# A Winograd filter's leftover channels: copied from the transformed tile into four 32-row tiles, instead of from the raw tile into two 64-row tiles

## Time and profile before

| | |
|---|---|
| median of 3 runs | 13046.61 us (13036.51 to 13055.05) |
| the profiled execution's own time | 13046.61 us |
| its span in the profile | 13044.8 us |
| mean granted TensorE clock | 0.982 |
| busy share of the span: PE, DVE, ACT, POOL | 95%, 64%, 42%, 36% |
| the third layer's filters, first to last | 5219.3 to 9748.2 us of the span |
| DMA engines over the third layer, mean share | 61% |

### The profile page before, as it was taken

How to read it: one execution, slowest core, us unless ns; L and a number is a source line. 1 busy time by engine, 2 the same in 40 slices (tenths; PEclk the granted TensorE clock), 3 DMA queues, 4 the chain that set the end, 5 groups by cost and what they waited for, 6 DMA issues and landing times. The chain is left out here.

```text
span 13044.8 us, 315786 instructions
## 1 busy us (share of the span) xinstructions
PE 12434.4 (95%) x126170; PEld 8455.1 (65%) x126170; DVE 8394.4 (64%) x17482; ACT 5423.2 (42%) x11157; POOL 4731.3 (36%) x3557
## 2 busy tenths in 40 slices
PE   7999899899989998999999999999998999999998
PEld 6877433577767776555555555555547777787777
DVE  0000677433335544888888888888887777777777
ACT  0000111211223333444444444444446666666666
POOL 0000222000000154666666666666653343333343
PEclk9999999999999999999999999999999999999999
DMA  4333556883754597666666666666642222222222
GB/s 128 133 133 130 135 153 160 160 154 70 153 126 151 155 228 184 83 85 86 84 85 85 85 86 84 85 85 85 86 75 63 52 51 52 52 52 52 53 51 49
DMA packets 2310007, 1323.92 MB, mean 101 GB/s; under 512 B 1872228, under 2 KB 2219867, under 8 KB 2222959
## 3 DMA queue, kind: packets, MB, share of 16 engines
q1 hardware_dynamic: 2041484, 1201.47, 46.4%
q10 hardware_dynamic: 267232, 104.65, 3.4%
HBM read 648.72 MB, written 450.74 MB: 84 GB/s over the span
## 5 line engine op out<-in xcount | busy, mean ns | idle before, releaser
L1581 PE MATMUL l_m<-l_wa,l_pix 128*128 128x288 f32 x8192 | 2263.6, 416 | 39.8 <-DVE l_qkv L1770 22.0
L1439 POOL TENSOR_TENSOR l_qkv<-l_qkv,l_copies 128x576 f32<-128x576 f32 x1024 | 1437.4, 1404 | 1727.5 <-DVE l_qkv L1773 1366.1
L1581 PEld LDWEIGHTS l_m<-l_wa,l_pix 128*128 128x128 f32 x8192 | 1454.3, 190 | 799.0 <-issue 370.9
L1285 PE MATMUL l1h_ps<-l1h_ring,l1h_w 96*96 96x256 f32 x6120 | 1327.4, 379 | 50.1 <-ACT l1h_ring L1233 47.0
L1056 PE MATMUL l1v_ps<-l1v_rows,l1v_w 96*96 96x256 f32 x6120 | 1325.3, 378 | 33.5 <-ACT l1v_rows L1029 33.5
L1429 POOL TENSOR_TENSOR l_pix<-l_raw 128x516 f32<-128x516 f32 x1024 | 1299.2, 1269 | 24.7 <-DMA l_raw<-l_raw 24.7
L2091 PEld LDWEIGHTS l_e<-k_ident,l_turn 128*112 128x112 f32 x9900 | 1084.4, 134 | 254.0 <-issue 128.7
L2091 PE MATMUL l_e<-k_ident,l_turn 128*112 128x128 f32 x9900 | 1162.5, 276 | 88.7 <-DVE l_out L2253 83.0
L1285 PEld LDWEIGHTS l1h_ps<-l1h_ring,l1h_w 96*96 96x96 f32 x6120 | 999.1, 163 | 378.4 <-issue 47.4
L1269 POOL TENSOR_TENSOR l1h_columns<-l1h_blocks,l1h_ring 96x2048 f32<-96x2048 f32 x64 | 356.0, 5585 | 2419.8 <-DVE l1h_ring L1318 2419.8
L1056 PEld LDWEIGHTS l1v_ps<-l1v_rows,l1v_w 96*96 96x96 f32 x6120 | 990.8, 162 | 367.6 <-issue 32.5
(11 more groups left out here) (245 smaller groups left out, 22745.3 us busy)
## 6 DMA issues: line engine op xcount, KB each, us to landing
l0a_x<-x_px_dram SPq DMA_DIRECT2D x128, 1176.0 KB, 5.1
l0b_x<-x_in_dram SPq DMA_DIRECT2D x128, 493.8 KB
l_raw<-l_raw SPq DMA_DIRECT2D x128, 483.6 KB, 7.1
l_raw<-x_dram SPq DMA_DIRECT2D x1280, 48.0 KB, 3.7
l_x<-x3p_dram SPq DMA_DIRECT2D x132, 384.0 KB
l_out<-x_dram SPq DMA_DIRECT2D x528, 96.0 KB
out_dram<-l_out SPq DMA_DIRECT2D x132, 384.0 KB
x_dram<-l0b_out ACTq DMA_DIRECT2D x256, 193.5 KB, 3.1
```

The costliest lines, as they stand in the source:

```text
L1285: last = nc.tensor.matmul(ps[g][0:C2, 0:GI * V], w[:, kernel, s, :], ring[:, g, before % DEEP, :, s:s + V], start=(s == 0), stop=(s == 2))
L1439: nc.gpsimd.tensor_tensor(q, q, copies[:, g % 2, 1:2, :].broadcast_to([128, 2, OUTC]), ALU.add)\
L1581: last = nc.tensor.matmul(bank[i][:, 0:OUTC], pix[:, k, i, first:first + 128], wa[:, b, i, :], start=True, stop=(i in (1, 2)))
```

```diff
@@ window_rows
-    for _ in range(2):
-        b += [(32 + ch, 2, dy) for dy in range(3) for ch in range(16)] + [(C, dx, dy) for dy in range(3) for dx in range(3)]
-        b += [(None, None, None)] * (HI - 57)
+    for i in range(4):
+        b += [(32 + ch, 2, i) for ch in range(16)] + [(C, dx, i) for dx in range(3)]
+        b += [(None, None, None)] * (32 - 19)
@@ stage_l2, load
                 if n >= NR:
                     sp.wait_ge(pix_out, 8 * (n - NR + 1))
                     sp.wait_ge(mid_in[(n - NR) % NX], 32 + 32 * ((n - NR) // NX))
-                    sp.wait_ge(left_in[(n - NR) % 2], 128 + 128 * ((n - NR) // 2))
@@ stage_l2, copy_left
-            def copy_left(n):
-                sp.wait_ge(loaded[n % NR], 160 + 160 * (n // NR))
-                if n >= 2:
-                    sp.wait_ge(conv_done, 32 * (n - 1))
-                last = raw[HI + 32:HI + C, n % NR, :].rearrange("p (r w) -> p r w", w=PW)
-                for h in range(2):
-                    for dy in range(3):
-                        first = h * HI + 16 * dy
-                        sp.dma_start(left[first:first + 16, n % 2, :].rearrange("p (r w) -> p r w", w=PW)[:, :, 0:W],
-                                     last[:, h + dy:h + dy + R - 1:2, 1:W + 1]).then_inc(left_in[n % 2], 16)
-                    sp.dma_start(left[h * HI + 48:h * HI + 58, n % 2, :],
-                                 D["k_rim"][h, :, (n % NBLK) * RUN:(n % NBLK + 1) * RUN]).then_inc(left_in[n % 2], 16)
+            def copy_left(n, half):
+                sp.wait_ge(pix_out, 8 * n + 4 * (half + 1))
+                first, end = half * HALF, (half + 1) * HALF
+                for i in range(4):
+                    sp.dma_start(left[32 * i:32 * i + 16, n % 2, first:end - 1],
+                                 pix[HI + 32:HI + C, n % 2, i, first + 1:end]).then_inc(left_in[n % 2][half], 16)
+                    sp.dma_start(left[32 * i + 16:32 * i + 20, n % 2, first:end],
+                                 D["k_within"][i, :, (n % NBLK) * RUN + first:(n % NBLK) * RUN + end])\
+                        .then_inc(left_in[n % 2][half], 16)
@@ stage_l2, SyncE's order
             for n in range(2):
                 shift_columns(n)
-            copy_left(0)
             load(2)
+            for half in range(2):
+                copy_left(0, half)
             for n in range(N):
-                if n + 1 < N:
-                    copy_left(n + 1)
                 if n + 3 < N:
                     load(n + 3)
                 if n + 2 < N:
                     shift_columns(n + 2)
+                if n + 1 < N:
+                    copy_left(n + 1, 0)
                 if n >= 1:
                     store(n - 1)
+                if n + 1 < N:
+                    copy_left(n + 1, 1)
@@ stage_l2, filters
                 if g == 0:
-                    pe.wait_ge(pix_out, 8 * n + 4 * half + 4)
-                if g == 0 and half == 0:
-                    pe.wait_ge(left_in[k], 128 + 128 * (n // 2))
+                    pe.wait_ge(left_in[k][half], 128 + 128 * (n // 2))
...
+                def centre(i):
+                    return nc.tensor.matmul(bank[i][:, 0:OUTC], pix[:, k, i, first:first + 128], wa[:, b, i, :],
+                                            start=True, stop=False)
+
+                def rest(i):
+                    rows = slice(32 * i, 32 * i + 20)
+                    return nc.tensor.matmul(bank[i][:, 0:OUTC], left[rows, k, first:first + 128], wb[rows, b, :],
+                                            start=False, stop=True)
                 for i in (1, 2, 0, 3):
                     if 4 * p + g > 0:
                         pe.wait_ge(freed[i], 4 * p + g)
-                    last = nc.tensor.matmul(bank[i][:, 0:OUTC], pix[:, k, i, first:first + 128], wa[:, b, i, :],
-                                            start=True, stop=(i in (1, 2)))
-                    if i in (1, 2):
-                        last.then_inc(conv_done, 1)
-                for i in (0, 3):
-                    rows = slice(i // 3 * HI, i // 3 * HI + 58)
-                    nc.tensor.matmul(bank[i][:, 0:OUTC], left[rows, k, first:first + 128], wb[rows, b, :],
-                                     start=False, stop=True).then_inc(conv_done, 1)
+                    centre(i)
+                for i in (1, 2, 0, 3):
+                    rest(i).then_inc(conv_done, 1)
@@ stage_l2, VectorE's prologue
-            nc.vector.tensor_scalar(gl[:], dwb[:], sign[:, 0:1], None, ALU.mult)
-            nc.vector.tensor_scalar(bl[:], bdw[:], sign[:, 0:1], None, ALU.mult)
+            nc.vector.tensor_scalar(gl[:, 0, :], dwb[:, 0, :], gk[:, 0:1], None, ALU.mult).then_inc(mixed, 1)
+            for k in range(1, 3):
+                dve.wait_ge(mixed, k)
+                nc.vector.scalar_tensor_tensor(out=gl[:, k, :], in0=dwb[:, k, :], scalar=gk[:, k:k + 1], in1=gl[:, k - 1, :],
+                                               op0=ALU.mult, op1=ALU.add).then_inc(mixed, 1)
```

More of the change, by code:

```diff
@@ L146, in shape_constants @@
         image[s, 1:H + 1] = col[s]
-    rim = np.ones((2, 10, H // 2, PW), np.float32)
-    for h in range(2):
-        for dy in range(3):
-            rim[h, 3 * dy:3 * dy + 3] = image[:, h + dy:h + dy + H:2]
-    c["k_rim"] = rim.reshape(2, 10, H // 2 * PW)
-    c["k_sign"] = np.repeat(np.array([[1], [-1]], np.float32), HI, axis=0)
+    first, second, third, fourth = (image[:, k:k + H:2] for k in range(4))
+    within = np.zeros((4, 4, H // 2, PW), np.float32)
+    for i, part in enumerate((first - third, second + third, third - second, second - fourth)):
+        within[i, 0:3] = part
+    within[1, 3] = 1
+    c["k_within"] = within.reshape(4, 4, H // 2 * PW)
+    gk = np.zeros((128, 3), np.float32)
+    for i, g in enumerate(((1, 0, 0), (0.5, 0.5, 0.5), (0.5, -0.5, 0.5), (0, 0, 1))):
+        gk[32 * i:32 * i + 32] = g
+    c["k_gk"] = gk
     f = np.zeros((64, 64), np.float32)
@@ L232, in lay_out @@
     w = i["L2_conv_w_dw"][:, 0]
[L233 to L239, removed]
+    dwa, dwb, bdw = (np.zeros(n, np.float32) for n in ((128, 3, C6), (128, 3, C6), (128, C6)))
+    for p, (ch, dx, _) in enumerate(window_rows()):
+        if ch is not None:
+            (dwa if p < 128 else dwb)[p % 128] = w[:, :, dx].T
+    bdw[32 + 19] = i["L2_conv_b_dw"]
     d["l2_dwa"], d["l2_dwb"], d["l2_bdw"] = dwa, dwb, bdw
@@ L1362, in before_qkv @@
             return early[0:parts, used[0] - width:used[0]]
-        win, bdw, sign = before_qkv(C + 1, OUTC), before_qkv(128, OUTC), sb("sign", [128, 1])
-        dwb, gl, bl = (before_qkv(128, OUTC) for _ in range(3))
-        dwa, ga = (before_qkv(128, n * OUTC).rearrange("p (t o) -> p t o", o=OUTC) for n in (3, 4))
+        win, bdw, gk = before_qkv(C + 1, OUTC), before_qkv(128, OUTC), sb("gk", [128, 3])
+        dwa, dwb, ga, gl = (before_qkv(128, n * OUTC).rearrange("p (t o) -> p t o", o=OUTC) for n in (3, 3, 4, 3))
         e1, e2 = before_qkv(C + 1, 256), before_qkv(C + 1, 256)
@@ L1391, in stage_l2 @@
         mid_in = [sem(f"mid_in{k}") for k in range(NX)]
-        left_in = [sem(f"left_in{k}") for k in range(2)]
+        left_in = [[sem(f"left_in{k}{half}") for half in range(2)] for k in range(2)]
         pix_out, conv_done, m1_out, m2_out, m0_out, m3_out, qkv_out = (
@@ L1464, in _ @@
         def _(sp):
-            cs = ((win, "l2_w"), (dwa, "l2_dwa"), (dwb, "l2_dwb"), (sign, "k_sign"), (bdw, "l2_bdw"), (e1, "k_e1i"), (e2, "k_e2i"),
+            cs = ((win, "l2_w"), (dwa, "l2_dwa"), (dwb, "l2_dwb"), (gk, "k_gk"), (bdw, "l2_bdw"), (e1, "k_e1i"), (e2, "k_e2i"),
                   (a, "k_a"), (cinv, "k_c"), (gb, "l2_gb"), (bout, "l2_bout"), (norm["sel"], "k_sel3"))
@@ L1750, in _ @@
                                            op0=ALU.mult, op1=ALU.add).then_inc(halved, 1)
-            nc.vector.tensor_scalar(gl[:], dwb[:], sign[:, 0:1], None, ALU.mult)
-            nc.vector.tensor_scalar(bl[:], bdw[:], sign[:, 0:1], None, ALU.mult)
+            nc.vector.tensor_scalar(gl[:, 0, :], dwb[:, 0, :], gk[:, 0:1], None, ALU.mult).then_inc(mixed, 1)
[3 more added lines that the diff above has]
+                                               op0=ALU.mult, op1=ALU.add).then_inc(mixed, 1)
             nc.vector.tensor_scalar(wout[:, 1, :], wout[:, 0, :], -1.0, None, ALU.mult).then_inc(mixed, 1)
             dve.wait_ge(halved, 3)
-            dve.wait_ge(mixed, 1)
+            dve.wait_ge(mixed, 4)
             for b in range(B):
@@ L1759, in _ @@
                     nc.vector.tensor_tensor(wa[:, b, i, :], m0[:, 0:OUTC], factor, ALU.mult)
-                nc.vector.tensor_tensor(wb[:, b, :], m1[:, 0:OUTC], gl[:], ALU.mult).then_inc(masked, 1)
+                nc.vector.tensor_tensor(wb[:, b, :], m1[:, 0:OUTC], gl[:, 2, :], ALU.mult).then_inc(masked, 1)
                 dve.wait_ge(masked, b + 1)
-                nc.vector.tensor_tensor(wb[:, b, :], wb[:, b, :], bl[:], ALU.add).then_inc(w_ready, 1)
```

(1 more changed line is left out.)

## The result

| | before | after |
|---|---|---|
| median | 13050.83 us (13036.51 to 13068.17, 4 runs) | 13139.14 us (13131.61 to 13142.27, 4 runs) |
| ratio, 95% interval | | 1.0066 (1.0049 to 1.0084) |
| span of the profiled execution | 13044.8 us | 13143.1 us |
| one block of the third layer's filters | 35.38 us | 36.01 us |

The change costs 88 us, or 0.66%: slower, as forecast, and inside the range, but 88 us where 198 were forecast.

A forecast was written before the change was run, and what follows sets the result against it. TensorE was taken to bound the kernel. Per block, +1.0 us for switches, -0.3 absorbed and +0.8 stall made 1.5; over 128 blocks 192 us, +6 at the start: +198, 13245 us, range 13110 to 13420.

The forecast's parts named there:

- four strips beside each other: TensorE's four 20-row matmuls run side by side in two passes, keeping the 0.59 us phase plus about 0.01 a group.
- spectrum let in behind the small matmuls: On TensorE, the spectrum would start 0.70 us behind the small matmuls in each group.
- all eight switches, before anything is absorbed: TensorE's change of tile height before the spectrum, 0.19 us in each of eight groups: 1.52 us a block.
- waits absorbed (GpSimd's and VectorE's): TensorE's waits for both engines' additions swallow part of the switches: 1.52 falls to 1.0, then -0.3 us a block.
- late counts: m1 and m2 complete only after the small matmuls, so ScalarE's two copies wait about 1 us longer; costed at nothing.
- stall for `left`: Filters 0 wait once a block for the first half of `left`, issued behind `mid`: 0.8 us, bounds 0 and 1.8.
- The switch back: Going from 32-row to 64-row tiles at the spectrum costs 0.09 us plus 0.08 for its weights in the open.
- The first rival: The switch from 32 to 64 rows is free and only the stall stays: +147 us, 13194; chance 12%.
- The second rival: The four strips do not run side by side: 13747 us if two at a time, 13400 on partial loss; chance 10%.
- I take half of it as absorbed, -0.3.: Half of TensorE's waits for VectorE's addition absorb added time, -0.3 us a block, bounds 0 and -0.56.
- the third rival: TensorE does not set the period; VectorE's chain does, and TensorE's additions fall into its waits: 13053 us; chance 9%.
- The start: At the layer's start, `left` for block 0 comes behind ten issues, so filters 0 start some 6 us later, once.

The follow-up runs named there:

- pad1: Kernel before, plus two 112-column matmuls ahead of each spectrum's wait for GpSimd, no change of tile height: 13098.26 us, ratio 1.0032.
- no_stall: Changed kernel with the first half of `left` issued ahead of SyncE's wait for the residual: 13121.92 us, ratio 1.0053 to the kernel before.
- rows64: Changed kernel with each small matmul widened from 20 to 52 rows in a 64-row tile, zero weights for the other strip: 13411.28 us, ratio 1.0269.
- pad1_late: Kernel before with pad1's padding and the counts for m1 and m2 given only by the first leftover matmul: 13117.63 us, ratio 1.0050.
- pad2: Kernel before with twice the padding of pad1 ahead of each spectrum: 13283.59 us, ratio 1.0168.
- later_left: Changed kernel with the first half of `left` issued later still, behind two stores: 13565.62 us, ratio 1.0388 to the kernel before.

## Why the prediction was right in its sign and wrong in its size

In us a block:

| term | forecast | measured |
|---|---|---|
| four strips beside each other | 0.01 a group | 0.01 (0.77 against 0.76) |
| spectrum let in behind the small matmuls | 0.70 | 0.70 |
| all eight switches, before anything is absorbed | 1.52 | 1.47 |
| waits absorbed (GpSimd's and VectorE's) | -0.8 | -1.24, by pad1 |
| late counts, and waits that stay (no_stall: 35.80 - 35.61) | 0 | +0.19 |
| stall for `left` (36.01 - 35.80) | +0.8 | lasts 0.40, costs 0.21 |
| sum | 1.5 | 0.63 |

*The switch back.* Right, to the hundredth, and by the mechanism: let in at 0.70, weights open, streaming at 0.78. That it is the height of the tile, not the number of matmuls or the transfers, is shown by rows64: it has the same eight small records and the same transfers, keeps the spectrum's height, and pays by passes alone. pad1_late shows that nothing else is needed: nearly the same time, added without any strip, gives the same block. The first rival, a free switch, is out, and with it the rule of the Trainium skill, "TensorEngine Tiling (Array Packing)", Key Properties, stands for 32 to 64 rows too: it gives the drain, this trace its 0.09 us and the weights' 0.08.

*The four strips.* The second rival is out: four at once, in two passes. For the 3.07 times of the Trainium skill, "TensorE: Matmul & The Clock Gate", Part 3, this trace shows no loss beyond 0.01 us in a phase of two passes.

*"I take half of it as absorbed, -0.3."* This step failed first. With GpSimd's part I had taken off 0.8, and I had counted 1.2 us of waits in the same rows. I kept half of VectorE's (0.28), and where the spectrum streamed at 0.85 before and streams at 0.78 now, in two groups, I put the gain at nothing (0.07 each). pad1 shows 1.24 us gone, pad2 that nothing is left after it. VectorE's largest wait, 0.44 us once a block, is more than the 0.195 that pad1 adds to one group, and it went all the same, so the time added in the groups ahead of it counts too. The reason that I gave for keeping half, VectorE's own work of 85% of the time, did not bind. So the third rival was half right: TensorE alone does not set the period of the kernel before, as 1.24 us a block of its time is waiting for others, and added time is free up to that. This is shown for time spread over all groups; time added at one place is here only in the stall, of which half is paid.

*"I take a stall of 0.8 us a block."* This failed too. Two of its terms were off, in opposite directions. The eight issues end later than I had (the last starts 5.85 us after the first to `mid`, in the mean, not 5.4), and they land sooner: 1.8 us from the last issue to filters 0, not 2.6. The 2.6 came from the layer's start, with TensorE's first wait of the layer; in the loop there is none like it. And a stall of 0.40 costs 0.21: it stands one group ahead of the waits for VectorE and GpSimd, so it replaces waits that come back when it goes (no_stall). In the changed kernel it is the only wait left: 35.61 + 0.40 is the measured 36.01. later_left shows the other end: where all waits are gone, the added lateness is paid in full, and 1.5 us a block for the stretches at the lower clock come on top.

*The late counts*, costed at nothing, cost 0.06 us a block alone and 0.13 on top of the padding (35.83 - 35.70), 8 to 17 us: small, but not nothing once TensorE has no slack. That in the changed kernel they are behind the 0.19 us that stay without the stall is argued from the same place in the block and the like size; no run took them out of it.

*The start*: +6 forecast; filters 0 moved by 6.3, counted from the layer's first instruction. The forecast missed by 110 us: 75 by the stall (0.8 - 0.21), 55 by the absorption (1.24 - 0.8), and some 20 the other way by the late counts and the waits that stay.

Left open: which of ScalarE's two late copies delays the second group of the block; it was not tried. Nor does any run say why the clock fell behind 52 of the 85 stalls of later_left and not behind the others: the mean stall is 2.49 us in the first and 2.50 in the second.

## What to carry to other kernels

Count a bound engine's waits before you price what is added to it: here, time spread over all groups was free up to the sum of those waits, and only the rest was paid; a padding of known length is a cheap way to measure that sum. A small matmul can cost more by its tile's height than by its size: between neighbours of another height it paid a drain and its successor's weights, here 0.18 us, nearly as much as 112 columns of two passes (0.195). And a transfer moved behind a producer is priced by the whole row of issues in front of it, not by its own.

## What the runs showed of the hardware

Four 32-row strips writing four PSUM banks over all 128 columns run at the speed of two 64-row tiles (0.77 against 0.76 us for two passes of 288 columns of float32). Changing from 32 to 64 rows costs what changing between 128 and 64 does, some 0.1 us (0.109 later let in, 0.01 of it for the longer phase), and 0.075 for the next weights in the open on top. Two store issues of SyncE's took 0.81 us behind the transfers to `left` and 2.08 us behind the larger ones to `mid`. Of 85 stalls of 2.0 to 3.4 us, once in a block of 39, 52 were followed by 3.4 to 10.2 us of TensorE at the lower granted clock (0.96 in the mean instead of 1.00); stalls of 0.2 to 0.8 us in the changed kernel left it at 1.00 through the whole loop.
